# One block for layer norm, first projection, adjacency and first convolution, with rows loaded two tiles at a time

## What is computed

```python
def _L0_gnn_ref(X, W, edge_src, edge_dst, edge_vals):
    Z = jnp.matmul(X, W)
    msg = Z[edge_src] * edge_vals[:, None]
    agg = jax.ops.segment_sum(msg, edge_dst, num_segments=X.shape[0])
    return jax.nn.relu(agg)

x = x + _L0_gnn_ref(_layernorm(x, axis=-1), L0_gnn_W, src, dst, edge_weight)
x = x + _L0_ffn_ref(_layernorm(x, axis=-1)[None], ...)   # attention, then 64 experts
x = x + _L1_gnn_ref(_layernorm(x, axis=-1), edge_index, ...)
x = x + _L1_ffn_ref(_layernorm(x, axis=-1)[None], ...)
```

## Time and profile before

| | |
|---|---|
| median of 3 runs | 1520.57 us (1516.29 to 1524.45) |
| span of the profiled execution, first to last instruction | 1515.1 us |
| PE, DVE, ACT, POOL busy | 94%, 49%, 31%, 15% of the span |
| mean granted TensorE clock | 0.976 of full speed |
| first product tile begins, last product tile is copied | 28.77, 67.63 us |
| first product of weights in the adjacency (L503) | 75.31 us |
| first product of the first convolution (L638) | 219.26 us |

### The profile page before, as it was taken

How to read it: one execution, slowest core, us unless ns; L and a number is a source line. 1 busy time by engine, 2 the same in 40 slices (tenths; PEclk the granted TensorE clock), 3 DMA queues, 4 the chain that set the end, 5 groups by cost and what they waited for, 6 DMA issues and landing times. The chain is left out here.

```text
span 1515.1 us, 24614 instructions
## 1 busy us (share of the span) xinstructions
PE 1431.1 (94%) x8028; PEld 921.8 (61%) x8029; DVE 736.7 (49%) x1546; ACT 470.4 (31%) x1153; POOL 226.3 (15%) x355
## 2 busy tenths in 40 slices
PE   7999999999989999999998999999899999889969
PEld 3488874455457777777455666666445555656642
DVE  7299966572157777777563222222250011633421
ACT  4299970021045555555111111111350012201111
POOL 2033330000000000000212222222330000012224
PEclk8999999999999999999999999999999999789998
DMA  5000000020000000000525999999630000823326
GB/s 150 0 1 0 0 28 0 0 84 0 0 29 2 2 2 2 1 2 1 156 68 174 326 324 322 319 322 325 179 83 0 0 0 0 286 54 118 125 92 181
DMA packets 94020, 142.39 MB, mean 94 GB/s; under 512 B 13245, under 2 KB 50515, under 8 KB 93823
## 3 DMA queue, kind: packets, MB, share of 16 engines
q1 hardware_dynamic: 69267, 97.52, 20.9%
q0 software_dynamic: 14976, 26.81, 6.4%
q10 hardware_dynamic: 9708, 17.12, 3.4%
HBM read 115.09 MB, written 26.29 MB: 93 GB/s over the span
## 5 line engine op out<-in xcount | busy, mean ns | idle before, releaser
L915 DVE TENSOR_REDUCE b_row_max<-ps 125x1 f32<-125x1251 f32 x80 | 116.4, 1455 | 60.0 <-PE ps L814 60.0
L1169 PEld LDWEIGHTS ps<-b_r 128*128 128x128 f32 x1024 | 124.3, 192 | 34.0 <-issue 32.5
L1169 PE MATMUL ps<-b_r 128*128 128x78 f32 x1024 | 122.2, 272 | 1.1 <-DVE b_r L1231 1.1
L1178 PE MATMUL ps<-b_r 128*78 128x512 f32 x256 | 121.6, 598 | 0.0
L503 PE MATMUL ps<-b_r 125*125 125x160 f32 x660 | 118.3, 315 | 0.0
L475 ACT ACTIVATE b_r<-b_r 125x125 f32<-125x125 f32 x330 | 107.8, 389 | 14.9 <-DVE b_r L427 10.6
L1215 ACT ACTIVATE b_r<-ps,b_r 128x78 f32<-128x78 f32 x128 | 34.6, 322 | 229.0 <-PE ps L1169 229.0
L109 PE MATMUL ps<-b_ones_bf 125*128 125x512 bf16 x371 | 88.4, 398 | 12.9 <-PEq L1129 3.3
L814 PE MATMUL ps<-b_r 64*125 64x417 f32 (+1 forms) x480 | 94.9, 524 | 3.1 <-DVE ps L935 1.2
L848 PE MATMUL ps<-b_r 125*64 125x125 f32 x1600 | 94.7, 272 | 1.1 <-DVE b_r L875 1.1
L1073 POOL TENSOR_TENSOR b_x<-b_x,b_r 125x512 f32<-125x512 f32 x10 | 12.7, 1268 | 544.5 <-DVE b_r L1019 544.5
(11 more groups left out here) (259 smaller groups left out, 2268.0 us busy)
## 6 DMA issues: line engine op xcount, KB each, us to landing
b_r<-L_ffn_w SPq DMA_DIRECT2D x128, 512.0 KB
y<-b_r ACTq DMA_DIRECT2D x64, 156.0 KB
b_r<-L_ffn_W SPq DMA_DIRECT2D x2, 4096.0 KB, 20.1
y<-b_r ACTq DMA_DIRECT2D x24, 256.0 KB, 2.3
rows<-b_r SPq DMA_DIRECT2D x2, 2400.0 KB
out<-b_x SPq DMA_DIRECT2D x10, 240.0 KB
y<-b_r SPq DMA_DIRECT2D x1, 2048.0 KB, 12.4
b_x<-x SPq DMA_DIRECT2D x2, 960.0 KB
```

The source lines that it names most:

```text
L915: link(dve.tensor_reduce(T.row_max[:, slot:slot + 1], T.ps[:P, 3 * h:3 * h + 3, 0:CW], AX.XY, ALU.max))
L1169: last = pe.matmul(T.ps[:, 2 + r % 2, f * CAP:(f + 1) * CAP], T.ew1[r % WS][:, k, f * 128:(f + 1) * 128], T.ex_t[:, r % 2, k, :], start=(k ...
L1178: last = pe.matmul(T.ps[:CAP, 4 + r % 2, :], T.eh[:, r % 2, f, :], T.ew2[r % WS][:, f, :], start=(f == 0), stop=(f == FK - 1))
```

## The change

The three blocks become one, `graph_convolution`, so that two barriers go. All of their instructions are still there, except for the following.

1. Loads: x comes in 5 pieces of 2 tiles, and `w_a` is issued second, behind the first piece. The load of the next weight into `w_a` waits for the last product.
2. VectorE normalizes in pairs of tiles: moments of both, then both normalized.
3. TensorE turns a pair (`turn`) and multiplies tiles (`product`) in an interleaved order. The edges are turned behind tile 5. Fillers: 22 and 4 instead of 45, and none ahead of the adjacency (30 before).
4. ScalarE loads its tables of functions early, copies a turned pair in 2 instructions instead of 4 for a group, and zeroes nothing. GpSimd zeroes 5,000 words of `at`, VectorE the other 7,500 and all of `ct`, most of it between the edge work and the columns.
5. The steps ahead of a pass: 4 are done ahead of the loop (`next_window`, `next_cells`) and again at the end of a pass, 2 at its start (`begin_pass`). The constants are folded: cells count from 1 (`cell_iota` base 1), and two comparisons become one product of (rel - 15) and rel.
6. TensorE's loop of visits is not peeled and waits at the end of a pass for the last sums (`end_pass`), since no barrier does so now.

Outside of it only counters of semaphores are renumbered (`turns_before`), an unused semaphore goes, and GpSimd zeroes a small table `ids`.

```diff
-def prologue(nc, T, S, A):
+def graph_convolution(nc, T, S, A):
...
-    BY_ACT, BY_DVE = 7000, 4000
...
+    BY_POOL, FIRST = 5000, 8000
+    PAIRS = NT // 2
+
+    def visits(engine, name, body, before=None, after=None, peel=True):
...
-            if after:
+            if after and peel:
                 body(0, engine.snap(seen, min_val=0, max_val=NG * WINDOWS), True)
...
+        @block.sync
+            for i in range(PAIRS):
+                sp.dma_start(T.x[0:120, 2 * i:2 * i + 2], x_rows[0:120, 2 * i:2 * i + 2]).then_inc(S.x_loaded[i], 16)
+                if i == 0:
+                    sp.dma_start(T.w_a, A.L0_gnn_W.rearrange("(k p) n -> p k n", k=KD)).then_inc(S.w0_loaded, 16)
...
+            sp.wait_ge(S.z_done, NT)
+            sp.dma_start(T.w_a, A.L0_ffn_wk.rearrange("(k p) n -> p k n", k=KD)).then_inc(S.wk_loaded, 16)
...
+            dve.memset(at[:, BY_POOL:FIRST], 0.0).then_inc(S.sums_cleared, 1)
+            for i in range(PAIRS):
+                dve.wait_ge(S.x_loaded[i], 32)
+                for t in (2 * i, 2 * i + 1):
+                    row_moments(dve, link, T, T.x, t, S.z_var)
+                for t in (2 * i, 2 * i + 1):
+                    dve.wait_ge(S.z_std, t + 1)
+                    normalize(dve, link, T, T.rows_a, T.x, t).then_inc(S.z_rows, 1)
+            dve.wait_ge(S.starts_ready, 1)
+            prepare_edges(dve, link, T, S)
+            dve.memset(at[:, FIRST:], 0.0).then_inc(S.sums_cleared, 1)
+            dve.memset(ct, 0.0).then_inc(S.sums_cleared, 1)
+            edge_columns(dve, link, T, S)
...
+            def begin_pass(r):
+                dve.wait_ge(S.at_added, r * NG + 2)
+                dve.wait_ge(S.ct_added, r * NG + 2)
+                dve.wait_ge(S.pass_step, r * STEPS + 4)
+                dve.tensor_scalar(T.base_row[:], T.base_all[0:1, :], float(LAST_WINDOW), None, ALU.min).then_inc(S.pass_step, 1)
+                dve.scalar_tensor_tensor(out=T.cell_col, in0=T.rel_col, scalar=0.0, in1=T.cell_any,
+                                         op0=ALU.is_le, op1=ALU.mult).then_inc(S.pass_step, 1)
...
+            next_window()
+            next_cells(0)
+            dve.sem_inc(S.ct_added, 2)
+            dve.reg_mov(passed, 0)
+            dve.wait_ge(S.sums_cleared, 4)
+            visits(dve, "dve", body, begin_pass, end_pass)
...
+            roots(0)
+            turned(0)
+            roots(1)
+            product_row(0)
+            turned(1)
+            roots(2)
+            product_row(1)
...
+            act.wait_ge(S.columns_ready, 1)
             visits(act, "act", body, None, last_weights)
...
+            keep_busy(pe, T, 7, 22)
+            pe.wait_ge(S.ident_ready, 1)
+            turn(0)
+            keep_busy(pe, T, 7, 4)
+            pe.wait_ge(S.w0_loaded, 16)
+            product(0)
+            turn(1)
+            product(1)
+            product(2)
+            turn(2)
+            product(3)
+            product(4)
+            turn(3)
+            product(5)
+            turn_edges(pe, T, S)
+            product(6)
+            turn(4)
+            for t in (7, 8, 9):
+                product(t)
...
+            def end_pass(seen):
+                pe.wait_ge(S.ct_added, seen + 2)
+                pe.wait_ge(S.at_added, seen + 2)
...
-            keep_busy(pe, T, 7, 30)
-            visits(pe, "pe", body)
+            pe.wait_ge(S.z_copied, NT)
+            pe.wait_ge(S.columns_ready, 1)
+            visits(pe, "pe", body, None, end_pass, peel=False)
```

More of the change, by code:

```diff
@@ L121, in transpose_group @@
         if j >= banks:
[L122 removed]
+            pe.wait_ge(S.tiles_copied, turns_before(use) + j - banks + 1)
         for t in range(t0, t0 + n):
@@ L335, in adjacency @@
-def adjacency(nc, T, S, A):
-    def visits(engine, name, body, before=None, after=None):
+    BY_POOL, FIRST = 5000, 8000
+    PAIRS = NT // 2
+    def visits(engine, name, body, before=None, after=None, peel=True):
         count = engine.alloc_register(name + "_passes")
@@ L440, in last_counts @@
                     add_counts(sums, seen, i - 2)
[L442 to L462 removed]
+                dve.reg_add(passed, passed, STEPS)
@@ new lines, in end_pass @@
+                done = dve.snap(passed, min_val=STEPS, max_val=STEPS * WINDOWS)
+                dve.tensor_scalar(T.base_all, T.base_all, float(WD), None, ALU.add).then_inc(S.pass_step, 1)
+                dve.wait_ge(S.pass_step, done)
+                next_window()
+                next_cells(done)
+            link(dve.tensor_copy(lo_iota, T.lo_iota[:]))
+            link(dve.tensor_copy(cell_iota, T.cell_iota[:]))
+            next_window()
+            next_cells(0)
+            dve.sem_inc(S.ct_added, 2)
@@ new lines, in ffn_input @@
+            def ffn_input(t):
+                dve.wait_ge(S.xf_std, 2 * t + 1)
+                link(normalize(dve, link, T, T.rows_b, T.x, t))
+                row_moments(dve, link, T, T.rows_b, t, S.xf_var)
+                dve.wait_ge(S.xf_std, 2 * t + 2)
+                normalize(dve, link, T, T.rows_c, T.rows_b, t, T.affine[:, 0, :], T.affine[:, 1, :])\
+                    .then_inc(S.attn_rows, 1)
+            dve.wait_ge(S.affine_loaded, 32)
+            for t in range(NT):
+                residual(t)
+                ffn_input(t)
@@ new lines, in _, with roots, turned @@
+            act.preload_act_table(ACT.Sqrt)
+            def roots(i):
+                row_roots(act, T, (2 * i, 2 * i + 1), S.z_var, S.z_std)
+            def turned(i):
+                for h in range(2):
+                    act.wait_ge(S.tiles_turned, 2 * i + h + 1)
+                    act.activation(T.feats[:, 2 * h:2 * h + 2, 2 * i * P:2 * (i + 1) * P],
+                                   T.ps[:, 2 + h, 0:4 * P].rearrange("p (k n) -> p k n", k=2), ACT.Copy)\
+                       .then_inc(S.tiles_copied, 1)
@@ new lines, in product_row @@
+            def product_row(t):
+                act.wait_ge(S.z_done, t + 1)
+                act.activation(T.rows_a[:, t, :], T.ps[:P, t % 2, :], ACT.Copy).then_inc(S.z_copied, 1)
+            roots(0)
[5 more added lines that the diff above has]
+            product_row(1)
+            roots(3)
+            product_row(2)
+            roots(4)
+            act.preload_act_table(ACT.Copy)
+            turned(2)
+            product_row(3)
@@ L466, in copy_weights @@
+            product_row(4)
+            turned(3)
+            product_row(5)
+            product_row(6)
+            turned(4)
+            for t in (7, 8, 9):
+                product_row(t)
             def copy_weights(i, seen):
```

328 lines of the change are left out of this document (129 added, 199 removed).

## The result

The changed kernel takes 1499.03 us in the median of 4 runs (1498.17 to 1507.04), the kernel before 1520.78 (4 runs). The ratio is 0.9867, interval 0.9836 to 0.9897: 20 us faster, between 16 and 25. In a later series of five rounds the ratio is 0.9870, interval 0.9846 to 0.9895. (Two executions of the kernel before in later series, of 1933.64 and 2885.52 us, fell in a slow state and are in no ratio.)

The account below looks back on a forecast made before the run. Prediction: product tiles pace TensorE's start, and all visits hang on the first product of weights at 75.31. Gain 18.6 - 0.2 (pass end) - 1.0 (clock) = 17.4; 1520.6 - 17.4 = 1503.2 us, range 1496 to 1512, own case 1498 to 1509.

Parts of the forecast that it names:

- Loads: Start of the kernel: queued transfers land in order at 5.24 us a MB; first pair 6.2, weight 11.7, second pair 14.2.
- TensorE's chain: Turns and product tiles: from the second turn at 17.6, 36.3 us without waiting for rows, last product ending at 53.9.
- Clock: TensorE's pauses among the first products: slow clock costs between nothing and 2.6 us, taken as 1.0.
- The sum by the page's rule: Trainium skill's advice against gaps: up to one 2.6 us warming up at each of two places, gain 13.2 us, 1507.4.
- From the last product to the first visit: Copy, loop entry of 1.14 us and three scalings: 2.8 us instead of 8.3, first product of weights at 56.7.
- End of the pass: After the last visit: VectorE's five extra instructions are free; TensorE leaving the loop costs 0.2 us more.
- Visits: From first product of weights to first convolution: nothing changed, distance stays 143.95 us but for 0.2.
- anything behind the first convolution takes another time: Sign, code after the first convolution product: the forecast is wrong if any time there changes.
- The late pair: Rival: second pair of x lands at 17.1 and the clock falls twice; 1508.7 us, chance 0.16.
- transfers side by side: Rival, loads: transfers are served together, so the first weight lands at 22.0; 1510.8 us, chance 0.08.
- cold visits: Last rival: visits start and stay at low clock, each some 1.1 us longer; 30 visits give 1536, chance 0.04.
- A takeover by VectorE: Rival, before the visits: VectorE, 4 us ahead, sets the pace if zeroing is slower; 1509, chance 0.08 shared with ScalarE.

Follow-up runs that it names:

- x_wlast: Changed kernel with the first weight's load queued behind all five pieces of x; first product of weights at 64.91 us instead of 57.73.
- b_loads: Kernel before with only the changed loads: x in five pieces of two tiles, first weight second in the queue; ratio 1.0011 to the kernel before.
- after: Profile of the changed kernel itself; first product of weights at 57.73 us, next block at 296.66, span 1496.1.
- after2: Changed kernel profiled once more, unchanged; first product of weights at 57.74 us, span 1502.4, median of 6 runs 1499.95.
- x_early: Changed kernel with ScalarE's start credits and TensorE's read of the pass count moved ahead of last product work; first product of weights at 57.84 us.
- x_barrier: Changed kernel with its block split by a barrier before the first visit; first product of weights at 58.61 us instead of 57.73.
- x_barsteps: Changed kernel split by a barrier before the first visit, with iotas and four steps behind it; first product of weights at 59.92 us instead of 57.73.
- x_nosteps: Changed kernel without VectorE's five instructions preparing a further pass; visits 142.60 us instead of 143.09, next block at 294.27 us.
- x_warm: Changed kernel with 12 more fillers in the pause before the second turn; last copy at 54.10 us instead of 55.72, next block at 297.99.
- x_fill: Changed kernel with 12 fillers before the second turn, 7 behind the last product tile, no further-pass steps; ratio 0.9890 to the kernel before.
- b_nofill: Kernel before without the 30 fillers ahead of the visits; visits 144.91 us instead of 143.95.
- b_root: Kernel before with ScalarE's 7,000 words of zeros given to GpSimd and the root table loaded early; first product tile at 30.93 us instead of 28.77.

## Why the prediction was right, point by point

Forecast 1503.2 (1496 to 1512), measured 1499.0. That the first product of weights stands at 57.73, where the forecast has 56.7 and 1.0 for the clock, is partly luck: the second turn came 0.35 us late, the clock cost 0.7 more than the 1.0, and against them stand 0.2 in the chain and 0.8 in the entry.

- *Loads.* In order, at 5.24 us a MB. Forecast for the first pair 6.2, the weight 11.7, the second pair 14.2; measured 6.16, 11.58 and 14.48. x_wlast shows the order of service, b_loads that the loads alone are worth nothing.
- *TensorE's chain.* Second turn forecast 17.6, measured 17.95; nowhere later does it wait for rows. From the second turn to the last copy I had 36.3 us; where the clock stays full it takes 36.08 or 36.09 in the five profiles that have the order unchanged, and the last copy starts at 53.8 to 53.9 in the three without fillers; the forecast was 53.9. The cover of 1.6 us for the turned edges held: VectorE's edge work ends at 37.96, its turn begins at 39.43.
- *Clock.* I put 1.0 us, an average over a loss and none. In after, after2 and x_early the distance from the second turn to the last copy is 37.77 us (in x_early without the 0.78 of its own read), so each lost 1.7; x_barrier, x_barsteps and x_nosteps with a like pause lost nothing. The length of the pause does not decide it: the clock was lost behind 2.56 us in x_early and kept behind the longest, in x_nosteps:

```profile
17.70 1.07 PE L526 MATMUL ps<-b_ident,b_r 125*128 125x125 f32 x8 [3.07 <-DVE b_r L172]
```

  So the term comes out as 0 or 1.7. The Trainium skill, "TensorE: Matmul & The Clock Gate", section "What's actually happening", says that the place of a transition varies from run to run; these profiles agree. There is a sign of it in the fillers: in the three that lost the clock the first 22 take 6.55 to 6.79 us, in the three that kept it 7.32 to 7.68, so the clock had risen earlier in the losers. Six profiles don't prove that the one decides the other. For the 12 fillers of x_warm speaks best x_fill, whose first 22 took 6.65 us like the losers' and which kept the clock there. The two pauses that I took for harmless or half so (ahead of the visits, ahead of the convolution) also cost the clock in some profiles and not in others: 1.2 us ahead of the visits (x_warm), and 1.5 to 1.7 ahead of the convolution (x_warm, x_fill, x_barsteps: 97.4 to 97.5 us from there to the next block instead of 95.8). The sum by the page's rule, with two warmings up of 2.6 us each, was 1507.4; in the changed kernel's profile one fall of 1.7 us came, and none ahead of the visits.
- *From the last product to the first visit.* Forecast 2.8 us, measured 2.0. The term that was mis-sized is the entry into the loop: 1.14 us, taken from a row of VectorE. ScalarE's own entry is hidden behind its last copy: it scales 0.34 us after it. I also had VectorE ready at 51.4, 4 us ahead; it is ready at 55.48, 0.24 ahead, and its memsets end at 49.42, not by 46. Of the 4.1 us, 1.9 are there when the edge work ends (37.96 for 36.1): the fourth pair's roots came 1.51 us late behind the copy of product tile 1, where I had looked only at the last pair's. That too is the low clock, which held up the product: after2 and x_early have such waits (0.52 and 1.05, 1.54), the profiles with the full clock have none, and in x_nosteps the edge work ends at 36.02. Another 2.4 are two pauses of VectorE ahead of its memsets (1.12 and 1.25 us), of the same length within 0.01 in all ten profiles of the changed kernel and its variants. I had priced none, though the earlier trace rows show one of 0.78 ahead of L271; what they are stays open. The cover is used up, though it still holds.
- *End of the pass.* I charged 0.2 us for leaving the loop and called VectorE's extra steps free. They are not quite: beside them GpSimd's last adds take 0.83 instead of 0.50, and without them the visits are 0.4 to 0.5 us shorter (x_nosteps). I asked only who waits for VectorE, not who works beside it.
- *Visits.* Said to be unchanged; they are 0.86 us shorter in spite of these 0.45. VectorE's one-hots come every 1.25 us in both, but across the end of each ten visits, from the second ten on, it takes 1.63 instead of 1.76, and nine such places give 1.2. That this is TensorE's loop without the peeled copy was not tried; it stays open.
- *The size.* 17.4 forecast, 18.42 at the last row that the change can move, 19.0 in span, 20 by the ratio, 21.8 between the medians. The difference between the last four lies within the scatter behind that row. By that scatter of 12 us my sign "anything behind the first convolution takes another time" could not have been read from whole runs; the 95.8 us to the next block are unchanged. The range of 1498 to 1509 is not the plain sum of its four bounds, which would be 1495 to 1512.5; 1499.0 lies in both.
- *Rivals.* The late pair fell by its own row (14.48, not 17.1), though the fall of the clock that went with it came once; transfers side by side fell by x_wlast, cold visits by b_nofill. A takeover by VectorE did not come, but by the rows it stood 0.24 us away. One sum in the last rival was loose: at 1.1 us a visit the change is slower than before from 16 cold visits on, and from 23 it can be told from no change.

## What to carry to other kernels

Read from the trace in which order a queue is served and at which pace, and write products so that each can start when its own rows and its weight are there. The loads alone give nothing (b_loads); with all the rest but the weight last in the queue (x_wlast) the last copy is 4.2 us earlier than before instead of 11.3. When work is moved beside another engine's, ask besides who waits for it also which of the two is slowed while both run. And when edits of 1 to 2 us are to be told apart in a run that scatters by 4, read them from the last row that they can reach.

## What the runs showed of the hardware

- A float32 tensor_scalar of VectorE beside a long GpSimd memset took 4.42 us instead of 0.55 and ended 0.28 us after the memset; the mean and variance (L151) beside the same memset took their usual 0.68, and a tensor_scalar of 125x1 its usual 0.15 (b_root). In the changed kernel a tensor_scalar of 125x110 took 0.52 instead of 0.21, and GpSimd's adds 0.83 instead of 0.50, where the two met.
- A pause of TensorE of 1.8 to 2.7 us costs the full clock in some profiles and not in others where the code around it is the same; one of 3.07 us kept it. Behind such a pause the low clock cost 1.2 us in the visits, where VectorE sets the pace, and 1.5 to 1.7 us where TensorE does; behind 5.68 us of pause it cost 1.9 in the visits.
- A low clock of TensorE reached VectorE's list too: in the profiles where it fell, roots that stand behind a product copy came up to 1.5 us late; where it stayed full they came in time.
- A warming up by fillers ahead of the visits is worth 1.0 us (b_nofill), not its length.
